# State-space scan on one core: C products of some states by ScalarE on turned states

## What is computed

```python
def step(h, inp):
    d_t, B_t, C_t, x_t = inp
    dA = jnp.exp(d_t[..., None] * A)
    h = dA * h + (d_t * x_t)[..., None] * B_t[:, None, :]
    y = jnp.einsum('ben,bn->be', h, C_t)
    return (h, y)
_, ys = jax.lax.scan(step, h0, xs)
y = ys.transpose(1, 0, 2) + D_skip * xi
y = y * jax.nn.silu(z)
```

## Time and profile before

| | us |
|---|---|
| three runs | 717.34, 719.96, 719.98 |
| median | 719.96 |
| profiled execution, span from first to last instruction | 706.5 |
| VectorE busy in the span | 488.4 |
| TensorE busy | 567.1 |
| ScalarE busy | 388.9 |
| GpSimd busy | 329.1 |

### The profile page before, as it was taken

The page is one execution under the profiler, slowest core; times in us unless marked ns, Lnnn a source line. Parts: engine busy times, 40 slices in busy tenths (PEclk is TensorE's granted clock), DMA queues, the critical chain, the costliest instruction groups (busy, mean ns, idle before and its releaser), DMA issues.

```text
span 706.5 us, 11037 instructions
## 1 busy us (share of the span) xinstructions
PE 567.1 (80%) x3428; PEld 360.0 (51%) x3447; DVE 488.4 (69%) x1296; ACT 388.9 (55%) x618; POOL 329.1 (47%) x287
## 2 busy tenths in 40 slices
PE   3959789686776766598999899947789989988787
PEld 1413333243242222397989799923545545545466
DVE  4749999967989998535423655387677778887052
ACT  2666656575654454265766557524266556565741
POOL 5259989916986799222778323432012103112010
PEclk9979999987968998999999999966999999999999
DMA  5855555514676355200132201323103003000001
GB/s 140 300 162 145 154 178 158 155 42 143 204 248 202 111 162 139 78 28 16 52 108 69 80 17 42 98 82 89 28 3 105 10 2 108 3 3 1 2 16 46
DMA packets 50524, 65.92 MB, mean 93 GB/s; under 512 B 7730, under 2 KB 29250, under 8 KB 50210
## 3 DMA queue, kind: packets, MB, share of 16 engines
q1 hardware_dynamic: 45122, 59.27, 28.5%
q0 software_dynamic: 2496, 5.15, 2.0%
q10 hardware_dynamic: 2848, 0.78, 0.5%
HBM read 47.46 MB, written 9.52 MB: 81 GB/s over the span
## 4 chain that ended last, share of the span: by engine, by line
PE 32%; DVE 9%; issue 8%; POOL 5%; ACT 4%; ACTq 1%; DMA 0%; POOLq 0%; another core or an unknown queue 0%; DVEq 0%
PE ps L1621 30%; DVE arena L1541 3%; POOL moe_out L836 2%; ACT arena L1141 2%; POOL moe_rows L828 1%; PE ps L1917 1%; DVE x L1476 1%; DVE nb L1240 1%; DVE stats L1227 1%; POOL arena L881 1%; PE ps L1924 1%; ACT arena L1161 1%; ACTq L1131 1%; POOL arena L877 0%; ACT r L1141 0%
## 5 line engine op out<-in xcount | busy, mean ns | idle before, releaser
L1621 PE MATMUL ps<-arena 128*128 128x128 f32 (+10 forms) x2131 | 328.6, 331 | 51.3 <-DVE arena L1541 18.0
L1621 PEld LDWEIGHTS ps<-arena 128*128 128x128 f32 (+2 forms) x2150 | 210.4, 160 | 136.4 <-issue 56.6
L1621 PE MATMUL ps<-arena,ident 128*128 128x512 f32 x256 | 134.8, 669 | 52.1 <-DVE arena L1423 52.1
L1411 DVE TENSOR_TENSOR_SCAN arena<-ps,arena 128x512 f32<-128x512 f32 x128 | 149.3, 1208 | 14.8 <-ACT ps L1067 6.8
L1067 ACT ACTIVATE ps<-arena 128x512 f32<-128x512 f32 x128 | 87.3, 690 | 84.5 <-DVE arena L1411 79.6
L1541 DVE CUSTOM_DVE_ANT_0 arena<-ps,cmask 128x128 f32<-128x128 f32 (+3 forms) x256 | 111.5, 487 | 26.8 <-PE ps L1621 25.4
L851 POOL TENSOR_TENSOR arena<-arena 128x1024 f32<-128x1024 f32 x64 | 126.8, 2000 | 1.5 <-DVE arena L1411 1.0
L1621 PEld LDWEIGHTS ps<-arena,ident 128*128 128x128 f32 x256 | 51.3, 211 | 131.4 <-DVE arena L1423 78.5
L836 POOL DMA_INDIRECT moe_out<-arena,xT x46 | 44.8, 973 | 70.1 <-DVE arena L1565 57.5
L1141 ACT ACTIVATE arena<-ps 128x1024 f32<-128x1024 f32 (+3 forms) x86 | 57.1, 709 | 36.0 <-PE ps L1621 35.6
L1595 DVE TENSOR_TENSOR arena<-arena,ps 128x512 f32<-128x512 f32 x46 | 31.7, 688 | 64.4 <-PE ps L1621 46.9
(11 more groups left out here) (199 smaller groups left out, 621.4 us busy)
## 6 DMA issues: line engine op xcount, KB each, us to landing
arena<-bc_rows SPq DMA_DIRECT2D x128, 256.0 KB, 3.8
arena<-arena SPq DMA_DIRECT2D x64, 64.0 KB
arena<-arena SPq DMA_DIRECT2D x28, 128.0 KB, 2.5
moe_rows<-arena SPq DMA_DIRECT2D x2, 1495.0 KB, 11.9
arena<-moe_rows SPq DMA_DIRECT2D x8, 325.0 KB, 4.9
arena<-in_L_attn_a_Wg SPq DMA_DIRECT2D x8, 256.0 KB, 3.9
arena<-in_L_attn_a_Wu SPq DMA_DIRECT2D x8, 256.0 KB, 5.1
arena<-moe_out SPq DMA_DIRECT2D x4, 512.0 KB, 5.2
```

Source lines behind the costliest of these rows:

```text
L1411: V.tensor_tensor_scan(hst[:, g % STATES, e, :], bank(6 + e), dBx[:, g % RING, e, :], 0.0, ALU.mult, ALU.add).then_inc(s_scan, 1)
L1621: return T.matmul(o, l, rr, start=start, stop=stop)
```

## The change

The 16 states of a batch are now split three ways. GpSimd has n = 1, 5, 9, 13 in batches 0 and 1, 1, 5, 9 in batch 2 and none in batch 3. New are the turned states: 3, 6, 8, 11 in batches 0 and 1, 3, 6, 8, 10, 12 in batch 2, and 0, 2, ..., 12 in batch 3. VectorE has the rest: 8, 8, 8 and 9.

For a turned state, TensorE turns eight blocks of 128x128 (four token blocks j, two channel halves e) into bank 3, four at a time (`turn_state`). ScalarE scales each token block, 128x256, by C, which is one number per partition now (`scale_turned`), and writes it to hT0 or hT1. TensorE multiplies the scaled block with the identity in such a way that it comes out unturned, straight into the sum in banks 0 and 1 (`sum_turned`). The C values by token come from eight small turns at the first state of a half and one copy (`turn_c`, `c_by_token`).

In the order of work: TensorE does the first four turns of t at state t+1, the second four and the sums of blocks 0 and 1 at t+2, the sums of blocks 2 and 3 at t+3, each ahead of that state's `sum_up`. ScalarE does the scalings of t after the second decay of t+1, after the first and the second of t+2, and after the first of t+3.

Turned states need no C row, so that `spread_c` issues fewer transfers and slots are counted by the states that have a row. Bank 3 is taken, so `copy_c` has bank 2 alone and waits for VectorE's last product. The load of the first expert's weights also waits for the C turns, whose source lies beneath. Eight semaphores of the attention (`s_mp`) become two with running counts, and unused stretches of the arena hold ctok, hT0 and hT1; these hunks are left out below.

```diff
@@ -441,10 +447,14 @@
             return b * NS + n
-        ON_POOL, POOL_LAG, SUM_LAG = ((1, 3, 6, 8, 11, 13), (1, 3, 6, 8, 11, 13), (1, 3, 6, 8, 11, 13), (5, 10)), 2, 2
+        POOL_LAG, SUM_LAG = 2, 2
+        ON_POOL = ((1, 5, 9, 13), (1, 5, 9, 13), (1, 5, 9), ())
+        TURNED = ((3, 6, 8, 11), (3, 6, 8, 11), (3, 6, 8, 10, 12), (0, 2, 4, 6, 8, 10, 12))
         NST = NB * NS
         on_pool = [g for g in range(NST) if g % NS in ON_POOL[g // NS]]
-        on_dve = [g for g in range(NST) if g not in on_pool]
+        on_turn = [g for g in range(NST) if g % NS in TURNED[g // NS]]
+        on_dve = [g for g in range(NST) if g not in on_pool and g not in on_turn]
+        with_row = [g for g in range(NST) if g not in on_turn]
         sums = []
         for g in range(NST):
             if g - SUM_LAG in on_pool:
@@ -452,6 +462,18 @@
             if g in on_dve:
                 sums.append(g)
+        def row_slot(g):
+            return with_row.index(g) % CS
+        def row_count(g):
+            return 16 * (with_row.index(g) // CS + 1)
+        def turn_count(g):
+            return len([t for t in on_turn if t <= g])
         def pool_count(g):
             return len([p for p in on_pool if p <= g])
@@ -459,6 +481,15 @@
         def dve_count(g):
             return len([d for d in on_dve if d <= g])
+        scale_at = {}
+        for t in on_turn:
+            for j, (later, e) in enumerate(((1, 1), (2, 0), (2, 1), (3, 0))):
+                g = t + later
+                last_of_half = (t // NS // HB + 1) * NS * HB - 1
+                if g > last_of_half:
+                    g, e = last_of_half, CT
+                scale_at.setdefault((g, e), []).append((t, j))
         def mamba_in(h, c):
@@ -656,13 +688,17 @@
                 sp.dma_start(bs[:, g % BS, :], bc_rows[b, n:n + 1, :].to_broadcast([P, L])).then_inc(s_bs[g % BS], 16)
             def spread_c(g):
+                if g in on_turn:
+                    return
                 b, n = divmod(g, NS)
-                if g - CS in on_pool:
-                    sp.wait_ge(s_hp, pool_count(g - CS))
-                else:
-                    wait(sp, s_cp, dve_count(g - CS))
-                sp.dma_start(cs_rows[:, g % CS, :], bc_rows[b, NS + n:NS + n + 1, :].to_broadcast([P, L])
-                             ).then_inc(s_cs[g % CS], 16)
+                q = with_row.index(g)
+                if q >= CS:
+                    if with_row[q - CS] in on_pool:
+                        sp.wait_ge(s_hp, pool_count(with_row[q - CS]))
+                    else:
+                        sp.wait_ge(s_cp, dve_count(with_row[q - CS]))
+                sp.dma_start(cs_rows[:, q % CS, :], bc_rows[b, NS + n:NS + n + 1, :].to_broadcast([P, L])
+                             ).then_inc(s_cs[q % CS], 16)
             def store_rows(b):
                 sp.wait_ge(s_dts, b + 1)
@@ -856,12 +892,12 @@
                             G.tensor_tensor(dx[:, :, L:HL], delta[:, :, L:HL], xc[:, :, L:HL], ALU.mult).then_inc(s_dx, 1)
                         p = g - POOL_LAG
                         if p in on_pool:
-                            pool.wait_ge(s_cs[p % CS], 16 * (p // CS + 1))
+                            pool.wait_ge(s_cs[row_slot(p)], row_count(p))
                             pool.wait_ge(s_scan, CT * p + CT)
                             k = sums.index(p)
                             wait(pool, s_ys, k - SUMS + 1)
                             G.tensor_tensor(hC[:, k % SUMS, :, :], hst[:, p % STATES, :, :],
-                                            cs_rows[:, p % CS, :].unsqueeze(1).to_broadcast([P, CT, L]),
+                                            cs_rows[:, row_slot(p), :].unsqueeze(1).to_broadcast([P, CT, L]),
                                             ALU.mult).then_inc(s_hp, 1)
                         if h and c == 0 and n == 2:
                             powers(0, 2 * TB)
@@ -1058,9 +1094,26 @@
             for h in range(HB):
                 (inputs_0, inputs_1)[h]()
                 def copy_c(g):
-                    act.wait_ge(s_cs[g % CS], 16 * (g // CS + 1))
-                    wait(act, s_hc, dve_count(g) - 2)
-                    S.copy(bank(2 + dve_count(g) % 2), cs_rows[:, g % CS, :]).then_inc(s_cp, 1)
+                    act.wait_ge(s_cs[row_slot(g)], row_count(g))
+                    wait(act, s_hc, dve_count(g) - 1)
+                    S.copy(bank(2), cs_rows[:, row_slot(g), :]).then_inc(s_cp, 1)
+                def c_by_token(h):
+                    act.wait_ge(s_ct, h + 1)
+                    S.copy(ctok[:, :, :, :].rearrange("p c j n -> p (c j n)"),
+                           ps[:, 3, 0:HB * TB * 2 * NS]).then_inc(s_ctk, 1)
+                def scale_turned(g, j):
+                    b, n = divmod(g, NS)
+                    k = TB * (turn_count(g) - 1) + j
+                    act.wait_ge(s_ht, k // 2 + 1)
+                    wait(act, s_hy, k - TB + 1)
+                    S.activation((hT0, hT1)[j // 2][:, j % 2, :], ps[:, 3, CT * P * (j % 2):CT * P * (j % 2) + CT * P], ACT.Copy,
+                                 scale=ctok[:, b % HB, j, NS + n:NS + n + 1]).then_inc(s_hs, 1)
+                def after_decay(g, e):
+                    for t, j in scale_at.get((g, e), []):
+                        scale_turned(t, j)
                 def decay(g, n, c, e):
                     wait(act, s_scan, CT * (g - 1) + e + 1)
@@ -1072,9 +1125,13 @@
                     for n in range(NS):
                         g = state_of(HB * h + c, n)
                         decay(g, n, c, 0)
+                        after_decay(g, 0)
                         decay(g, n, c, 1)
+                        after_decay(g, 1)
                         if g in on_dve:
                             copy_c(g)
+                        if c == 0 and n == 1:
+                            c_by_token(h)
                         if c == n == 0:
                             row_copy(h, 1)
                             relu_abs(h, 1)
@@ -1092,6 +1149,7 @@
                             logits(0)
                         if g == ROUTE_AT["exp"]:
                             router_exp(0)
+                after_decay(state_of(HB * h + HB, -1), CT)
             S.preload_act_table(ACT.Silu)
             def clear_keys(b):
@@ -1406,13 +1464,15 @@
                         if g >= STATES:
                             if g - STATES in on_pool:
                                 dve.wait_ge(s_hp, pool_count(g - STATES))
+                            elif g - STATES in on_turn:
+                                dve.wait_ge(s_ht, 2 * turn_count(g - STATES))
                             else:
                                 dve.wait_ge(s_hc, dve_count(g - STATES))
                     V.tensor_tensor_scan(hst[:, g % STATES, e, :], bank(6 + e), dBx[:, g % RING, e, :], 0.0,
                                          ALU.mult, ALU.add).then_inc(s_scan, 1)
                 def weigh(g):
-                    if g in on_pool:
+                    if g not in on_dve:
                         return
                     k = sums.index(g)
                     dve.wait_ge(s_cp, dve_count(g))
@@ -1421,10 +1481,11 @@
                     if g == state_of(HB * h, 0):
                         dve.wait_ge(s_dl, HB * h + HB)
                     V.tensor_tensor(hC[:, k % SUMS, :, :], hst[:, g % STATES, :, :],
-                                    bank(2 + dve_count(g) % 2).unsqueeze(1).to_broadcast([P, CT, L]), ALU.mult).then_inc(s_hc, 1)
+                                    bank(2).unsqueeze(1).to_broadcast([P, CT, L]), ALU.mult).then_inc(s_hc, 1)
                 def gate(c):
-                    dve.wait_ge(s_ys, state_of(HB * h + c, NS))
+                    dve.wait_ge(s_ys, len([k for k in sums if k < state_of(HB * h + c, NS)]))
+                    dve.wait_ge(s_hy, TB * turn_count(state_of(HB * h + c, NS) - 1))
                     cs = slice(c * L, c * L + L)
                     dve.wait_ge(s_zs, 2 * HB * (h + 1))
                     V.tensor_tensor(zs[:, :, cs], bank(0, 2), (zs, zr)[h][:, :, cs], ALU.mult).then_inc(s_yg, 1)
@@ -1757,6 +1818,46 @@
                         last = mm(bank(e), ident[:], src[:, e, :], start=False, stop=(g % NS == NS - 1))
                     last.then_inc(s_ys, 1)
+                def turn_c(h):
+                    pe.wait_ge(s_dl, HB * h + 1)
+                    pe.wait_ge(s_dts, HB * h + HB)
+                    for c in range(HB):
+                        for j in range(TB):
+                            at = (TB * c + j) * 2 * NS
+                            last = T.transpose(ps[:, 3, at:at + 2 * NS], dts[RK:RK + 2 * NS, c, j * P:j * P + P],
+                                               ident[RK:RK + 2 * NS, RK:RK + 2 * NS])
+                    last.then_inc(s_ct, 1)
+                def turn_state(g, q):
+                    k = 2 * (turn_count(g) - 1) + q
+                    if q == 0:
+                        pe.wait_ge(s_scan, CT * g + CT)
```

(41 more changed lines are left out.)

6 lines of the change are left out of this document (3 added, 3 removed).

## The result

The changed kernel takes 734.33 us (median of 4 runs, 732.80 to 735.98), the kernel before beside it 719.97: ratio 1.0212, interval 1.0185 to 1.0239. It is slower by 14.4 us; forecast was 7.5.

What follows compares the result with a forecast made beforehand. VectorE's queue of scans and products was taken to set the pace in batches 0 to 2, with GpSimd's scatters also bounding batch 3. +9.1 + 2.6 - 4.2 = +7.5 gave 727.5 us; 8-in-10 range 713 to 737.

Steps and rivals of the forecast that it cites:

- The gain: Products taken off VectorE and GpSimd, all batches: -11.4 us if no stall came at all, giving 708.6 us.
- ScalarE stands in its queue: A turned state's first scaling waits for TensorE's turns, holding up later decays and VectorE's scan; 0.96 or 0.46 us before additions.
- The forecast's signs: Scaling waits of 10 us or more, scan idle time released by ScalarE from 6.8 to over 20, 44 products becoming 33.
- Half 0: Batches 0 and 1, from the scan of state 1 to the last product: 95.9 us becomes 105.0, +9.1.
- The price of one turned state: From VectorE's product of t-1 through to the next decay: 4.32 us, or 3.82 without the copy, against three scans' 3.36.
- Batch 3: From the scan at 232.31 to the last product: 53.9 us becomes 49.7, -4.2; GpSimd allows no more than -4.7.
- Batch 2: New stalls of 8.8 us replace earlier waits, and 2.24 of products go: +2.9, taken as +2.6.
- t=35: Turned state 35 in batch 2: 0.96 plus normalisation on ScalarE in state 36, a stall of 2.2 us.
- t=38, 40 and 42: Turned states in batch 2: stalls of 1.9 (input copies), 3.65 (GpSimd's sum and the router) and 0.5 us.
- Rival 2: TensorE at its slow clock after idleness: four turned states met there cost +9 us, 736 in all; chance 0.12.
- 13.5 lies around the span: Whole kernel: 719.96 us median less the 706.5 profiled span leaves 13.5 us, which the change does not touch.
- Counting by rates: Scalings on ScalarE against a product on VectorE: 0.52 us lost for each of 20 states, 10 us.

Runs made afterwards that it cites:

- run 5: Changed kernel without any turns, scalings or sums of turned states, so the output lacks their C products; 709.73 us, ratio 0.9885.
- run 6: Changed kernel with every turned-state instruction but no waits between ScalarE and TensorE for them, a constant tile standing in as data; 711.80 us, ratio 0.9904.

## Why the prediction was right and wrong

The direction and its mechanism were right, the size was half: +7.5 forecast, +14.4 measured, inside the range. Between the second profile of before and the one after lie 17.0 us, 9.5 more than forecast: 5.6 of them in batch 3, 3.4 in batch 2, and 0.5 in all other stretches together.

- **The gain:** 11.4 us forecast with no stall at all, 9.9 measured (run 5: 719.65 less 709.73).
- **ScalarE stands in its queue:** shown by run 6. The forecast's signs came true: over 10 us of waits at the scaling (35.6), over 20 of ScalarE's at the scans (35.5), 33 products. The Trainium skill says the same of ScalarE's queue ("TensorE: Matmul & The Clock Gate", section "Architectural detail: the array is 16× 32×32, not 1× 128×128": strictly first in, first out), and the trace agrees: ScalarE stood 8.90 us at one scaling, with the decays of state 50 behind it.
- **Half 0:** +9.1 forecast; +8.8 against the first profile, +9.2 against the second. The price of one turned state, built from the chain product, sum, turns, scaling, copy, decay, held place by place: in front of states 5, 10, 13 and 21, 2.26, 2.70, 1.79 and 2.65 were forecast, 2.00, 2.42, 1.58 and 3.04 came. The interpolated 0.47 for the scaling was 0.471.
- **Batch 3 is the step that failed:** "From the scan at 232.31 to the last product: 5.6 (five pieces of 1.12)". Five pieces of VectorE's time, with no stall counted at state 48, which is turned as well. Its turns stand behind gating and D skip, the same mechanism as everywhere else, and that cost 5.20; with the 0.65 by which the gap in front of state 52 (1.41) exceeds the steady 0.76, that is 5.85. The piece forecast at 5.6 took 10.92 (244.39 to 255.31), and -4.2 became +1.4. The rest of the term held: pairs lay 6.46 apart (260.17 to 266.63), forecast 6.56, and with the turns in time batch 3 takes 49.5, forecast 49.7.
- **Batch 2:** +2.6 forecast; +3.9 against the first profile, +6.0 against the second. The stalls counted here came to 9.0 where 8.8 was forecast, and that is luck. t=35 was priced at TensorE's high clock (2.2); its sum took 3.78 where 1.83 had been used, and the gap was 4.13. Those of t=38, 40 and 42 were 1.46, 3.01 and none, for 1.9, 3.65 and 0.5. Rival 2 had the mechanism of t=35, with four places and a chance of 0.12; it came beside the forecast, here and at the border, not in its place. What the count left out is VectorE's routing, shown above: its two steps make 0.8 us of the loss against the first profile and 1.9 against the second.
- **"13.5 lies around the span"** was a misreading of one short execution: 1.7 lies around the span after (734.43 and 732.7). It did no harm, as the sum is a difference to the median.
- **The longest gaps** were not all behind 8, 24 and 40 (2.42, 2.16, 3.01); those in front of 21, 37 and 50 were longer.
- **Counting by rates,** the forecast's second way to 10 us, came nearer to 14.4 for the wrong reason: run 6 has every scaling, turn and sum and is only 2 us behind run 5. The Trainium skill, "Perfetto Trace Analysis", section "Identifying the Most-Contended Engine", would have the engine with the highest occupancy optimised first. VectorE was relieved of eleven products here, and the time rose; in run 5, where nothing takes their place, it fell by 9.9.

Before's 2.1 us in batch 2 between its two profiles are the routing step shown above (1.70 and 0.59), the wait of 1.63 in the earlier trace rows, which was 0.86, and 0.2 in front of state 33. The 1.5 us between the halves lie between the gating and VectorE's next step: 6.95 us at a granted clock of 0.75 in the second profile of before, 5.45 at 1.00 after. Not settled: what made the granted clock differ there, and behind the last scan of the first profile, between executions of the same work.

## What to carry to other kernels

When work moves to engines with room, follow its handovers, not its totals: 20 states with two round trips between two in-order queues cost 22 us of waits here, while the work alone cost about 2. Count such a wait at the first item behind each border too, where other waits already stand in the queue. Before building all of a change, do the part where nothing stands in the way: here batch 3 alone, with the turns in front, beats both kernels.
